# Two layers of graph attention, GRU and sparse experts: orders at four joints, and the second layer's probability carried in the token's row

## The reference

```
x = x + gat(layernorm(x), adj)        # 1 head: softmax over neighbours of leaky_relu(s1 + s2), then elu
x = x + experts0(layernorm(x))        # 8 experts, 128 -> 512 -> 128, relu; top 2, softmax of the two scores
x = x + gru(layernorm(x), adj)        # 3 rounds: m = h W_i; aggr = A m; h = gru_cell(aggr, h)
x = x + experts1(layernorm(x))        # 16 experts, 128 -> 256 -> 128, silu(x w1) * (x w2); top 2 of softmax,
                                      # divided by their sum
```

## Time and profile before

| | us |
|---|---|
| median of the runs | 1142.51 |
| profiled execution, its own time | 1139.99 |
| its span | 1138.2 |
| PE busy | 984.0 (86%) |
| DVE busy | 768.5 (68%) |
| POOL busy | 599.1 (53%) |
| ACT busy | 586.7 (52%) |

### The profile page before, as it was taken

The page is one execution under the profiler, slowest core; times in us unless marked ns, Lnnn a source line. Parts: engine busy times, 40 slices in busy tenths (PEclk is TensorE's granted clock), DMA queues, the critical chain, the costliest instruction groups (busy, mean ns, idle before and its releaser), DMA issues. The chain is left out here.

```text
span 1138.2 us, 27212 instructions
## 1 busy us (share of the span) xinstructions
PE 984.0 (86%) x6880; PEld 807.3 (71%) x6881; DVE 768.5 (68%) x2985; ACT 586.7 (52%) x1485; POOL 599.1 (53%) x622
## 2 busy tenths in 40 slices
PE   4677775699999999759999999999995799999970
PEld 3666665599999999735555555555553799999970
DVE  3666766476666666437788888888875655555548
ACT  3777775334343434235556665666553344444445
POOL 2277777475555555500135554545445677766670
PEclk8777877699999999969999999999996899999995
DMA  9511111242222222130230321303011543333339
GB/s 229 198 48 46 49 47 59 72 112 75 70 70 70 72 70 66 51 110 1 73 89 24 96 67 53 103 21 128 24 36 36 127 112 110 93 94 87 92 133 370
DMA packets 109670, 99.10 MB, mean 87 GB/s; under 512 B 33424, under 2 KB 94480, under 8 KB 109328
## 3 DMA queue, kind: packets, MB, share of 16 engines
q1 hardware_dynamic: 92432, 62.83, 20.1%
q0 software_dynamic: 17152, 35.29, 9.3%
HBM read 55.44 MB, written 42.62 MB: 86 GB/s over the span
## 5 line engine op out<-in xcount | busy, mean ns | idle before, releaser
L1670 POOL DMA_INDIRECT result<-e_y,e_ids x280 | 279.0, 997 | 163.8 <-issue 79.1
L415 POOL DMA_INDIRECT queue<-rows,slots x256 | 262.9, 1027 | 173.2 <-issue 120.7
L1701 PE MATMUL e_ps_h<-e_xT,e_up_of 128*128 128x128 f32 x2240 | 276.4, 277 | 2.2 <-DVE e_hT L1814 1.8
L1701 PEld LDWEIGHTS e_ps_h<-e_xT,e_up_of 128*128 128x128 f32 x2240 | 264.1, 194 | 3.4 <-issue 2.6
L1716 PE MATMUL e_ps_y<-w_sb,e_hT 128*128 x1664 | 208.4, 275 | 0.0
L1716 PEld LDWEIGHTS e_ps_y<-w_sb,e_hT 128*128 128x128 f32 x1664 | 196.9, 192 | 0.2 <-issue 0.2
L1740 ACT ACTIVATE e_hT<-e_ps_h,b_sb 128x128 f32<-128x128 f32 x272 | 77.9, 369 | 112.8 <-PE e_ps_h L1701 111.1
L1771 DVE COPY e_up_of<-w_sb 128x512 f32 x280 | 112.1, 441 | 4.7 <-issue 0.6
L1799 DVE TENSOR_SCALAR e_hT<-e_ps_h,b_sb 128x128 f32<-128x128 f32 x272 | 76.4, 343 | 32.9 <-PE e_ps_h L1701 32.2
L1814 DVE TENSOR_TENSOR e_hT<-e_ps_h,e_gate 128x512 f32<-128x512 f32 x72 | 49.6, 689 | 69.6 <-ACT e_gate L1749 69.5
L1749 ACT ACTIVATE e_gate<-e_ps_h 128x512 f32<-128x512 f32 x72 | 43.0, 597 | 95.5 <-PE e_ps_h L1701 94.2
(11 more groups left out here) (213 smaller groups left out, 1785.4 us busy)
## 6 DMA issues: line engine op xcount, KB each, us to landing
xq<-queue SPq DMA_DIRECT2D x280, 64.5 KB
g_y<-result SPq DMA_DIRECT2D x20, 512.0 KB, 4.0
result<-e_y,e_ids POOLq DMA_INDIRECT x280, 2.4
x_res<-x SPq DMA_DIRECT2D x16, 256.0 KB, 3.7
w_sb<-w SPq DMA_DIRECT2D x2, 2048.0 KB, 11.9
queue<-rows,slots POOLq DMA_INDIRECT x256, 2.3
w_sb<-w SPq DMA_DIRECT2D x16, 256.0 KB
rows<-result SPq DMA_DIRECT2D x8, 512.0 KB, 8.1
```

The source lines that it names most:

```text
L415: pool.indirect_dma_start(out=queue, out_offset=bass.IndirectOffsetOnAxis(ap=c.slots[q][:, k, t:t + 1], axis=0), in_=c.rows[q][:, k, t, :] ...
L1670: pool.indirect_dma_start(out=result, out_offset=bass.IndirectOffsetOnAxis(ap=ids[at_down.k][:, t, :].bitcast(U32), axis=0), in_=y[at_down ...
L1701: last = pe.matmul(ps_h[b][:, t, q * P:(q + 1) * P], up_of[at_up.k % 4][:, t, q * P:(q + 1) * P], xT[at_up.k % 4][:, t, :], start=True, st ...
```

## The change

- **GAT to experts.** The products move from behind the last step of the stage to a place before group 14's rank matmuls. POOL issues AHEAD0 = 5 rows of group 14 in the stage, so 11 instead of 16 rows are late.
- **Experts to GRU.** ACT copies group 0's state between the normalisations of groups 0 and 1.
- **Steady pairs.** gap is computed on DVE behind MAX and not behind the slots, into two buffers. Both groups' probabilities stand at k = 5 behind gate_r; before, one group's stood there and the other's at k = 1 of the next pair.
- **GRU to experts.** In pair 7 the table stands at k = 4, ahead of group 12's route_vector_2, and tail_1 of group 14 in k = 5. POOL issues all of 12's rows and the first three of 13's before rstd of group 14, one between the two rstd, and two of group 14's at the end (AHEAD1 = 2), so 14 instead of 16 are late. TensorE makes the scores of group 15 (into another bank) before the ranks of group 14.
- **Probability in the row.** A row of the queue has 130 words instead of 129: ACT's sigmoids write the probability into the row, the experts copy it with the ids, and ACT's copy of y out of PSUM is scaled by it (layer 0's rows carry a zero there that is not used). In Finish, ACT's scaling goes and DVE makes two additions of 512 columns a group.

The diff, cut to its core (lines with ## name the function and engine):

```diff
+AHEAD0, AHEAD1 = 5, 2
...
-ROW = D + 1
+ROW = D + 2
...
## gat_and_routing, POOL
-                if g4 and not (type(g4.s) is int and g4.s >= NG - 2):
+                if g4 and not (type(g4.s) is int and g4.s == NG - 1):
                     wait(pool, VK, "slots", g4.s)
                     wait(pool, AC, "rows", g4.s)
                     alone(pool, c)
-                    queue_rows(pool, c, c.queue0, g4.b)
+                    ahead = AHEAD0 if type(g4.s) is int and g4.s == NG - 2 else TOPK * G
+                    queue_rows(pool, c, c.queue0, g4.b, 0, ahead)
...
## gat_and_routing, TensorE: products() is the loop of the last lines of the stage
+                if g3 and type(g3.s) is int and g3.s == NG - 2:
+                    products()
...
## route_best and route_vector_2, DVE
+    v.tensor_tensor(r.gap[b][:], r.top[b][:, :, 1], r.top[b][:, :, 0], ALU.subtract).then_inc(V.sem, 1)
-    if A:
-        wait(v, A, "p1", at.back(1))
-    v.tensor_tensor(r.gap[:], r.top[b][:, :, 1], r.top[b][:, :, 0], ALU.subtract).then_inc(V.sem, 1)
...
## gru_and_routing, POOL
+                    wait(pool, AT2, "p1", group)
...
-                    rows_of(even, 4, s_tok, u)
-                    rows_of(even, 5, s_aggT, u)
+                    if has_run:
+                        rows_of(even, 4, s_tok, u)
+                        rows_of(even, 5, s_aggT, u)
+                    else:
+                        for m in range(3):
+                            rows_of(odd, m)
                     rstd_and_shift(pool, c, tail_norm, VT, GT, AT0, group(n - 1, 0))
-                    rows_of(even, 6)
-                    rows_of(even, 7, s_aggT, u + 1)
-                    rows_of(odd, 0, s_r, u + 1)
+                    if has_run:
+                        rows_of(even, 6)
+                        rows_of(even, 7, s_aggT, u + 1)
+                        rows_of(odd, 0, s_r, u + 1)
+                    else:
+                        rows_of(odd, 3)
                     rstd_and_shift(pool, c, tail_norm, VT, GT, AT0, group(n - 1, 1))
-                    rows_of(odd, 1)
-                    rows_of(odd, 2, s_aggT, u + 2)
-                    rows_of(odd, 3, s_r, u + 2)
+                    if has_run:
+                        rows_of(odd, 1)
+                        rows_of(odd, 2, s_aggT, u + 2)
+                        rows_of(odd, 3, s_r, u + 2)
...
+                if has_tail and not has_run:
+                    for m in range(AHEAD1):
+                        rows_of((n - 1) * 2, m)
...
## gru_and_routing, TensorE, k = 2
+                if has_tail and has_run:
+                    tail_rank(pa[0])
                 if has_tail:
+                    tail_score(pa[1])
+                if has_tail and not has_run:
                     tail_rank(pa[0])
-                    if not has_run:
-                        wait(pe, VK, "carried", pa[0].s)
...
## gru_and_routing, ACT
-                    if k == 1 and has_tail and (type(n) is not int or n >= 2):
-                        tail_probs(group(n - 2, 1))
-
                     if k in (2, 3) and has_tail:
-                        tail_rows(pa[k - 2])
+                        tail_turned(pa[k - 2])
+                        if has_run:
+                            tail_rows(pa[k - 2])
                     if k in (1, 2) and has_tail:
                         norm_tail(pa[k - 1])
+                    if k in (2, 3) and has_tail and not has_run:
+                        tail_rows(pa[k - 2])
                     if k in (4, 5) and has_head:
                         norm_head(nx[k - 4])
+                    if k == 4 and has_head and not has_run:
+                        head(nx[0])
                     if k == 5 and has_tail and not has_head:
                         tail_probs(pa[0])
+                        tail_probs(pa[1])
                     if has_run:
                         gate_r(n, l, b)
                     if k == 5 and has_tail and has_head:
                         tail_probs(pa[0])
-                if not has_run and not has_head:
-                    tail_probs(pa[1])
-                if not has_run and has_head:
-                    head(nx[0])
...
## gru_and_routing, DVE
-                    if k in (0, 1) and has_tail:
+                    if k in (0, 1) and has_tail and (k or has_run):
                         tail_1(pa[k])
                     if k == 5 and has_tail and not has_head:
                         route_vector_2(v, c, r, VK, AT2, QT4, pa[1], E1)
...
                     if k in (0, 1) and has_tail:
                         tail_2(pa[k])
                         tail_ids(pa[k])
+                    if k in (2, 3) and has_tail:
+                        route_vector(v, c, r, VS, QT3, AT2, pa[k - 2], E1, c.gate1_b[:], QT4)
                     if k == 3 and has_tail and not has_run:
                         route_vector_2(v, c, r, VK, AT2, QT4, pa[0], E1)
-                    if k in (2, 3) and has_tail:
-                        route_vector(v, c, r, VS, QT3, pa[k - 2], E1, c.gate1_b[:], QT4)
+                    if k == 4 and n == pairs - 1:
+                        wait(v, VK, "carried", NG - 5)
+                        table_of_known(v, c, table, E1)
+                        v.drain()
                     if k == 4 and has_tail and has_run:
                         route_vector_2(v, c, r, VK, AT2, QT4, pa[0], E1)
+                    if k == 5 and n == pairs - 1:
+                        tail_1(group(n, 0))
...
-                    if k == 2 and n == pairs - 1:
-                        wait(v, VK, "carried", NG - 5)
-                        table_of_known(v, c, table, E1)
...
## experts, ACT
+                    act.wait_ge(ids_copied, at_down.done())
                     for t in range(PAIR):
                         act.activation(y[at_down.k][:, t, :], ps_y[at_down.k % 2][:, t * D:(t + 1) * D],
-                                       ACT.Copy).then_inc(y_copied, 1)
+                                       ACT.Copy, scale=ids[at_down.k][:, t, 1:2]).then_inc(y_copied, 1)
...
## experts, POOL: late groups, ((NG - 2, AHEAD), (NG - 1, 0))
-            for group in late:
-                queue_rows(pool, c, queue, group % TURN)
+            for group, first in late:
+                queue_rows(pool, c, queue, group % TURN, first)
...
## Finish
-    def scale(self, act):
-        c = self.c
-        for s in range(NG):
-            y = self.y[s % OUT_BUFFERS]
-            act.wait_ge(self.arrived[s % OUT_BUFFERS], (s // OUT_BUFFERS + 1) * 16)
-            for t in range(G):
-                last = act.activation(y[:, t, 1, :], y[:, t, 1, :], ACT.Copy,
-                                      scale=c.prob[:, 1, s * G + t:s * G + t + 1])
-            last.then_inc(self.scaled, 1)
+            xs = c.x[:, s * G:(s + 1) * G, :]
             v.wait_ge(self.arrived[s % OUT_BUFFERS], (s // OUT_BUFFERS + 1) * 16)
-            for t in range(G):
-                last = combine(v, c, y, t, 0, s)
-            last.then_inc(self.first_added, 1)
+            v.tensor_tensor(xs, y[:, :, 0, :], xs, ALU.add).then_inc(self.first_added, 1)
             v.wait_ge(self.first_added, s + 1)
-            v.wait_ge(self.scaled, s + 1)
-            xs = c.x[:, s * G:(s + 1) * G, :]
```

More of the change, by code:

```diff
@@ L390, in route_buffers @@
     r.slotf = sb(prefix + "slotf", [P, TOPK, G])
-    r.gap = sb(prefix + "gap", [P, G])
+    r.gap = [sb(prefix + f"gap{b}", [P, G]) for b in range(2)]
     r.egap = sb(prefix + "egap", [P, G])
@@ L770, in _ @@
                 v.memset(h[b][:, :, D:D + 1], 1.0)
+            for q in range(TURN):
+                v.memset(rows[q][:, :, :, D + 1:ROW], 0.0)
             for b in range(2):
@@ L979, in _, with products @@
             pe.wait_ge(wa_copied, 1)
+            def products():
+                pe.wait_ge(small_loaded, 16 * len(small_weights))
+                wait(pe, AT, "xnT", NG - 1)
+                wait(pe, AA, "pT", NG - 1)
+                wait(pe, AH, "h", NG - 1)
+                for l in range(LAYERS):
+                    last = pe.matmul((ps_t, ps_p, ps_h)[l][:, 0:3 * D], c.gnn_w[:, l * D:(l + 1) * D], c.w_ih[:],
+                                     start=True, stop=True)
+                last.then_inc(product_made, 1)
             def body(g0, g1, g2, g3, g4):
@@ L1044, in _ @@
             staged(pe, body)
-            pe.wait_ge(small_loaded, 16 * len(small_weights))
-            wait(pe, AT, "xnT", NG - 1)
-            wait(pe, AA, "pT", NG - 1)
-            wait(pe, AH, "h", NG - 1)
-            for l in range(LAYERS):
-                last = pe.matmul((ps_t, ps_p, ps_h)[l][:, 0:3 * D], c.gnn_w[:, l * D:(l + 1) * D], c.w_ih[:],
-                                 start=True, stop=True)
-            last.then_inc(product_made, 1)
 def load_group(sp, c, adj, at):
@@ L1212, in body @@
                     rows_of(even, 3, s_r, u + 5)
+                    if not has_head:
+                        for m in range(4, 8):
+                            rows_of(even, m)
```

(2 more changed lines are left out.)

48 lines of the change are left out of this document (25 added, 23 removed).

## The result

The changed kernel takes 1147.55 us (median of 5 runs, 1146.25 to 1149.17), the kernel before, run beside it, 1142.47. The ratio is 1.0055, with a 95% interval of 1.0044 to 1.0066: 0.55% slower. The forecast was 1143.1 and its range ended at 1147.5. The profiled execution has a span of 1144.5 us, against 1138.2.

A forecast was written before the change was run, and what follows sets the result against it. TensorE was taken to bound the experts and GRU, DMA the last stage, leaving the joints between stages. Terms -4.4 - 2.5 + 1.1 + 8.8 - 2.2 - 0.3 + 0.1 = +0.6 gave 1143.1 us, range 1138.0 to 1147.5.

The forecast's parts named there:

- Two memsets at the start: Start of the kernel: two added memsets cost +0.1 us.
- Joint B: Experts to GRU: the earlier state copy lets the aggregation start sooner; -2.5 us, bounds -2.96 to -1.65.
- R4: Rival at GAT to experts: something else, such as instruction queue fill, keeps the experts from starting earlier; 1147.5 us, chance 0.07.
- Joint A: GAT to experts: with the products moved, TensorE starts the experts earlier, at 211.6; -4.4 us, bounds -4.9 to -2.0.
- The steady pairs: GRU: two more small sigmoids on ACT ahead of g_tok cost 0.2 per pair; +1.1 us, bounds 0 to +1.2.
- Joint C: GRU to experts: the table's new place delays POOL's rows and rstd(14); +8.8 us, bounds +5.0 to +12.4.
- The late rows: Second layer's experts: 14 late rows instead of 16 remove both TensorE stalls; -2.2 us, bounds -2.9 to -1.0.
- the last stage: Last stage: DMA sets the pace, so only the last group's shorter arithmetic counts; -0.3 us, bounds -5.9 to 0.
- R1: Rival in the last stage: DVE, not DMA, sets the pace, so fewer DVE operations help; 1137.9 us, chance 0.13.
- R3: Rival in the GRU's tail: TensorE gets the full clock, together -2.8 us; 1140.3 us, chance 0.10.
- R2: Rival ahead of rstd(14): POOL's rows stretch beside DVE's two-input instructions, +3.6 us; 1146.7 us, chance 0.17.
- The wider row: Queue rows of 130 words, not 129: 17,152 packets change by 4 bytes, at a cost of 0.

The follow-up runs named there:

- e1: The kernel before with only four small memsets added on DVE ahead of the GAT loop: 1147.68 us against 1141.14, ratio 1.0066.
- e12: The kernel before with two memsets of h's last columns on DVE cut into six that write the same: 1148.01 us, ratio 1.0071.
- e2: The changed kernel with its four memsets of the rows' last word on POOL instead of DVE: 1138.56 us, ratio to the kernel before 0.9987.
- e13: The kernel before with two memsets of h's last columns on DVE cut into three that write the same: 1139.03 us, ratio 0.9993.
- e5: The changed kernel with AHEAD1 = 0, so no row of group 14 is issued in the GRU stage: 1147.92 us.
- e8: The changed kernel without the addition of the first expert's result on DVE in the last stage: 1146.23 us.
- e10: e7 with the second group's probabilities back at k = 1 of the next pair in the steady pairs: 1130.23 us, ratio 0.9897.
- e4: The changed kernel with group 12's probabilities in pair 7 taken on ACT at k = 3, not k = 5: 1146.02 us.
- e3: The changed kernel with the table of known groups back at k = 2 of pair 7: 1140.07 us, ratio to the kernel before 1.0009.
- e7: The changed kernel with memsets on POOL, table at k = 2, group 12's probabilities early and rows free, AHEAD1 = 0: 1130.95 us, ratio 0.9918.

## Why the prediction was wrong

**The step that failed** is the last and smallest one: "Two memsets at the start: +0.1". I counted instructions of 0.1 us, and asked only what they take, not where they put the code behind them. It also says two, where DVE has four and POOL one. What they measured is +6.7 us of GAT's loop in the changed kernel, 6.7 to 9.4 in the traces of all eight kernels with four more memsets on DVE ahead of it (e1 and e12 on the kernel before), and nothing where they are on POOL (e2) or where it is one (e13, 1.2 shorter). The +0.6 at the start can't be told from chance: there the traces differ by -1.2 to +1.1. Without this term the same working gives +0.5, and the trace of e2 -1.2. The miss in the sum would have been larger still had joint B not brought 2.1 more than forecast. The cause, waiting for code at the loop's branch, rests on the place of the gap, the ten transfers, two of which start in each gap, and the edge between one and four instructions. The Trainium skill, "Runtime: NRT & Kernel Launch", section "Instruction fetch mechanics", says that a taken branch whose target isn't in the window of code held forces a fetch before execution goes on. These traces agree with 3.9 to 4.7 us at such a branch, where the kernels without the four memsets have 0.3 to 0.4. I had not weighed that rule. R4 did name the filling of the instruction queue, but at the jump to the experts and not in a loop; that the time came out at R4's 1147.5 is chance.

**Joint A** was right: TensorE started at 211.22 in e2 against 211.6 forecast. The clock's give-back was 0.8 and not 0.25.

**Joint B** was right in its mechanism: g_tok behind the second group's normalisations was late next. Its lower bound of -2.96 left the clock out, and the changed kernel's -4.6 lies beyond it. Alone it brought -3.0. How much joints A and B move with no edit shows in e5 and e8, whose code there is that of the changed kernel: A is -5.3 and B -3.5 in both, where the changed kernel has -4.0 and -4.6.

**The steady pairs** were right, +0.9 for +1.1, and e10 takes it away again by the step that was named.

**Joint C** was right in size, to 0.1 us, and partly by luck. The table, the 6.5 us of idle and POOL's queue ahead of rstd(14) were as described. But I had overlooked the wait on the probabilities for row (12, 0), which the diff shows; the row that it releases comes 4.2 us before the row (12, 3) that I used (864.88 against 869.05 in e4), with three rows of 1.27 more behind it, and these two ways end within 0.1 us of each other. And the 0.4 for two rows at the stage's end was 1.9 (e5). The chain from rstd(14) to the experts still took 17.9 us (878.91 to 896.77) for the 18.1 forecast, because without the two rows it takes 15.95 where I had 17.7.

**The late rows** and **the last stage** were right: -2.3 for -2.2, and the DMA engines set the end (e8). R1 and R3 had nothing to them. R2 had little: of the eleven rows two took 1.23 and 1.09, the others 0.95 to 0.96. The wider row moved 0.38 MB more (99.48 against 99.10) and not the 0.07 of 17,152 packets, and e2's GAT shows no cost of it.

## What to carry to other kernels

An instruction that is added ahead of a loop has two prices: its own, and that of the code it moves. After any edit of an engine with loops, compare the packets of the instruction queue and look for idle time put down to "issue" at the loop's turns; if both grew, put the instructions on another engine before judging the change. Where two waits end with the same step, an experiment that takes one away shows nothing; take both.

## What the runs showed of the hardware

- Between one and four more instructions ahead of it, DVE's loop began to fetch code at its turns: 3.9 to 4.7 us of idle at each of two branches, ten transfers of 8 KB, and a loop longer by 6.7 to 9.4 us, in eight kernels. Four nops in that place did not move the code.
- After the same idle of 2.72 us at the same place, TensorE's granted clock fell to 0.50 in one kernel and stayed at 1.00 in another (e3). That, and the time at which it rises again at the GRU's start, moved kernels with no edit there by up to 1.8 us (e12).
- POOL's first row of group 14 was followed by the next only 2.59 us later, and not about 1.3, in every kernel, whether it stood ahead of the stage's end or behind it (893.71 to 896.30 in the changed kernel, 877.39 to 879.98 in e7). Why is open.
